# Attention with a mixture of experts, one core: waits that are already satisfied left out of the queues, and one bias folded into another at the start

## The chip, the cores and the metric

One NeuronCore of a Trainium2 chip runs the whole program. The metric is the device time of one execution in microseconds (us); lower is better.

## The reference, cut to what matters

Eight batches of 512 rows by 128 columns. Each row is normalised, and the result `xn` goes through two branches that are added to `x`:

```
xn = layernorm(x)
out = x + attention(xn) + ffn(xn)

attention: q, k, v = xn @ W_qkv (16 heads of 64), rotary embedding on q and k, causal softmax, @ W_out
ffn:       q, k, v = xn @ Wq + bq, xn @ Wk + bk, xn @ Wv + bv      (16 heads of 8)
           ctx = softmax(q k' / sqrt(8)) v
           attn_out = ctx @ Wo + bo
           x2 = xn + layernorm(attn_out) * g1 + be1
           gate = softmax(x2 @ Wg + bg); the two best of 8 experts: sum of gate * (x2 @ We + bexp)
           ffn = x2 + layernorm(that) * g2 + be2
```

The softmax rows of the FFN's attention sum to one. So `bv`, which is added to each row of v, comes out of that attention unchanged, and `ctx @ Wo + bo` is the same with v lacking its bias and `bo` replaced by `bo + bv @ Wo`.

## The kernel before

The work of each batch is cut into steps, each with a short name: `proj` (projection of 128 columns of q or k), `raw`, `swap`, `rope`, `hi` and `lo` (its way through ScalarE, a DMA and GpSimd), `sc` (scores), `max`, `exp`, `tp` and `tq` (transposes of the weights), `tpe` and `tqe` (their copies), `pv`, `rT`, `div` and `ao` for the causal attention; `fqk`, `fsm`, `fmax`, `fmT`, `fst`, `fexp`, `fv`, `fpv`, `fT` for the FFN's; `wo`, `gate`, `moe` for the rest. A table of times (`START`, `PERIOD`, `SHIFT`, `FIRST`, `LAST`) is written out by hand, and sorting it gives each engine a fixed order: 1250 steps for TensorE, 1166 for ScalarE, 1074 for VectorE, 432 for GpSimd. The steps of neighbouring batches are interleaved. The order is the same in both kernels.

Engines meet through semaphores. Every kind of step has one (`done[kind]`), which a step raises by one when it ends. `after(kind, ...)` gives the semaphore and the value that it has when the named step is done:

```python
def after(kind, *key):
    if (kind,) + key not in COUNT:
        return begun, 1
    return done[kind], COUNT[(kind,) + key]
```

A step waits with `engine.wait_ge(*after(...))` for each of its inputs and for whoever last used the buffer that it overwrites. On TensorE there are also the waits for the PSUM banks: `BEFORE[x]` names the steps that free them (lines 1181 to 1187). An instruction of an engine takes one wait with it; the others stand in instructions of their own in the engine's queue, up to two waits in each. The trace calls these EVENT_SEMAPHORE, and their line is that of a wait.

Many of these waits name a value that the same engine has already waited for. The step `fmT` waits for eight `fmax` of one semaphore, one after the other; `inv` for six `exp`; `sc` for `hi` and `lo` of q and of k, though GpSimd makes each `lo` after its `hi`; and the second `fpv` of a group waits for `fexp` values that an earlier bank wait covered.

Products with more than half precision are made of three matmuls (`split3`: high by high, low by high, high by low, lines 1166 to 1168) and, where there is a bias, a fourth of 128 rows by 128 columns that adds one row of the tile `biases`, picked by a column of `pick` (line 1170). Four steps use it: `fv` (bias `bv`, 4 such matmuls per batch), `wo` (`bo`, 4) and `moe` (`bexp`, 8 of 512 columns).

The start: SyncE loads x, the constants, Wq and Wk, the biases of q and k (line 679) and, when GpSimd has cleared `raw_bias`, `bexp`, `bv` and `bo` twice each (line 686). TensorE then does `xT`, `tt`, `proj`, `tb` (a transpose of the q and k biases, line 1196), `fqk`, `fv`. VectorE does `ln`, `turn`, `str`, `xn`, `strl`, `wl`, `xl`, `wl`, `sml`, `qkb` (lines 972 and 976, from the result of `tb`), `bia` (lines 990 to 993, `pick` and `biases`), `wel` (line 997), `fqkl` (line 1013).

Of the kernel before, what the change touches and what calls it, by code (L numbers as in the profile page):

```python
# [14 lines left out]
P = 128  # L15
# [17 lines left out]
BIAS = {"bexp": 0, "bv": 2, "bo": 3}  # L33
# [502 lines left out]
def build(nc, x, w_qkv, w_out, wq, bq, wk, bk, wv, bv, wo, bo, g1, be1, g2, be2, wg, bg, we, bexp, table, rope, out):  # L536
    with ExitStack() as ctx:
# [32 lines left out]
        spare = sb("spare", [P, 1])  # L570
        warm = sb("warm", [P, 1])
# [62 lines left out]
        columns_loaded = sem("columns_loaded")  # L634
        causal_loaded = sem("causal_loaded")
# [35 lines left out]
        def _(sp):  # L671
# [20 lines left out]
            for x_ in ORDER["SP"]:  # L692
                kind, b = x_[:2]
                if kind == "swap":
# [3 lines left out]
                    sp.wait_ge(*after("raw", b, c, k))  # L698
                    sp.wait_ge(*after("rope", old, older // 2, older % 2))
                    for r in range(2):  # L700
                        sp.dma_start(swapped[r:P:2, n % 2], raw[1 - r:P:2, n % 3]).then_inc(swap_done[n % 2], 16)
                elif kind == "store":
                    sp.wait_ge(*after("out", b))
# [8 lines left out]
        def _(pool):  # L712
# [16 lines left out]
            for x_ in ORDER["POOL"]:  # L729
                kind, b = x_[:2]  # L730
                if kind in ("rs0", "rs1", "rs2"):
                    n = int(kind[2])
                    pool.wait_ge(*after(("ln", "ln1", "ln2")[n], b))
                    nc.gpsimd.tensor_tensor(rstd[:, n], spread[:, n], power[:], ALU.pow).then_inc(done[kind], 1)
                elif kind == "rope":
                    c, k = x_[2:]
                    n = (b * NC + c) * 2 + k
                    pool.wait_ge(*after("raw", b, c, k))
                    if n == 0:
                        pool.wait_ge(*after("tab", 0))  # L740
# [6 lines left out]
                elif kind == "hi":  # L747
                    c, k = x_[2:]
                    n = (b * NC + c) * 2 + k
                    pool.wait_ge(*after("rope", b, c, k))  # L750
                    pool.wait_ge(*after("sc", *ring(2, b, c, NC), 2))
                    nc.gpsimd.tensor_copy(qk_h[:, c % 2, k], raw[:, n % 3]).then_inc(done["hi"], 1)  # L752
                elif kind == "lo":
                    c, k = x_[2:]
                    n = (b * NC + c) * 2 + k
                    pool.wait_ge(*after("hi", b, c, k))
                    nc.gpsimd.tensor_tensor(qk_l[:, c % 2, k], raw[:, n % 3], qk_h[:, c % 2, k].bitcast(F32),  # L757
                                            ALU.subtract).then_inc(done["lo"], 1)
                elif kind in ("x2", "out"):
                    n = 0 if kind == "x2" else 2  # L760
                    pool.wait_ge(*after("nm1" if kind == "x2" else "nm2", b))
# [11 lines left out]
                    else:  # L773
                        pool.wait_ge(*after("res", b))
                        nc.gpsimd.tensor_tensor(x_in[:, b % XB], branch[:], x_in[:, b % XB], ALU.add).then_inc(done["out"], 1)
                elif kind == "res":
                    pool.wait_ge(*after("x2", b))
                    pool.wait_ge(*after("yadd", b, 1))
                    nc.gpsimd.tensor_tensor(x_in[:, b % XB], xn[:, b % 2], x_in[:, b % XB], ALU.add).then_inc(done["res"], 1)

        @block.scalar
        def _(act):
# [12 lines left out]
            for x_ in ORDER["ACT"]:  # L795
                kind, b = x_[:2]
                if kind == "tab":
                    act.wait_ge(*after("tt", 0))
# [13 lines left out]
                elif kind == "xh":  # L812
                    act.wait_ge(*after("xT", b))
                    act.wait_ge(*after("proj", b - 2, NC - 1, 1))
                    act.wait_ge(*after("fqk", b - 2, G - 1))
                    act.wait_ge(*after("v", b - 2, T - 1))
                    nc.scalar.copy(xt_h[:, b % 2], bank_of(("xT", b))).then_inc(done["xh"], 1)
                elif kind == "fvc":
                    act.wait_ge(*after("fv", b))
                    act.wait_ge(*after("fpv", b - 1, G - 1, T - 1))  # L820
                    nc.scalar.copy(fv[:, :, :, 0:FD], bank_of(("fv", b)).rearrange("p (t h d) -> p t h d", t=T, d=FD))\
                        .then_inc(done["fvc"], 1)
                elif kind == "fqkh":
                    g = x_[2]
                    act.wait_ge(*after("fqk", b, g))
                    act.wait_ge(*after("fst", *ring(2, b, g, G), T - 1))
                    if b == 0:
                        act.wait_ge(*after("qkb", 0))
# [4 lines left out]
                elif kind == "fexp":  # L833
                    g, i, r = x_[2:]
                    act.wait_ge(*after("fst", b, g, i))
                    if b == 0:
                        for n in range(3):
                            act.wait_ge(*after("wl", 0, n))
                    old, older = ring(FP, b, g * T + i, G * T)
                    act.wait_ge(*after("fpv", old, older // T, older % T))  # L840
                    nc.scalar.activation(fpt[:, ((b * G + g) * T + i) % FP, 2 * r:2 * r + 2].rearrange("p h n -> p (h n)"), bank_of(("fst", b, g, i), 2 * r, 2),  # L841
                                         ACT.Exp, scale=1.0 / math.sqrt(FD)).then_inc(done["fexp"], 1)
                elif kind == "fo":
                    g = x_[2]
                    act.wait_ge(*after("fpv", b, g, T - 1))
                    act.wait_ge(*after("fT", *ring(1, b, g, G)))
                    nc.scalar.copy(fo[:], bank_of(("fpv", b, g, 0))).then_inc(done["fo"], 1)
                elif kind == "ch":
                    act.wait_ge(*after("cT", b))
                    act.wait_ge(*after("moe", b - 1, T - 1))  # L850
                    nc.scalar.copy(ct_h[:], bank_of(("cT", b))).then_inc(done["ch"], 1)
                elif kind == "x2h":
                    act.wait_ge(*after("x2T", b))
                    act.wait_ge(*after("wo", b))
                    nc.scalar.copy(ct_h[:], bank_of(("x2T", b))).then_inc(done["x2h"], 1)
                elif kind == "gexp":
                    act.wait_ge(*after("gsub", b))
                    act.wait_ge(*after("moew", b - 1, T - 1))
# [566 lines left out]
```

## Time and profile before

| | |
|---|---|
| median of 3 runs | 1279.72 us (1278.18 to 1283.24) |
| the profiled execution | 1279.87 us |
| its span, first to last instruction | 1277.9 us |
| busy: TensorE, VectorE, ScalarE, GpSimd | 1156.8, 928.2, 892.0, 818.0 us |
| mean granted TensorE clock | 0.981 |

The profiled execution is 1.97 us longer than its span, and 0.15 us longer than the median. In the profile PE is TensorE's matmul row, PEld its row of weight loads (which overlap matmuls), DVE is VectorE, ACT ScalarE, POOL GpSimd, SP SyncE; a name with a q behind it (PEldq, ACTq) is that engine's queue of instructions. Matmuls are pipelined, so the busy time of PE is larger than the time in which it could do no more. A number like L1267 is a line of the kernel.

### The profile page before, as it was taken

What the parts mean: (1) busy time and instruction counts of PE and PEld (TensorE: products, weight loads), DVE (VectorE), ACT (ScalarE), POOL (GpSimd) and SP (SyncE); (2) the same over time, 40 slices, a digit from 0 to 9 for tenths busy, and PEclk for the clock granted to TensorE, in tenths of its full rate; (3) what the DMA queues carried; (4) which work ended last, traced back from release to release, by engine and by line L of the source; (5) the groups of instructions that cost most, each with busy time, mean ns of one, the idle gap of its engine ahead of it and who ended that gap; (6) DMA issues with size and microseconds to landing.
All of it is one profiled execution on the core that took longest, in us unless ns stands there. A gap on an engine that the chain in (4) does not pass through costs nothing.

```text
span 1277.9 us, 28127 instructions
## 1 busy us (share of the span) xinstructions
PE 1156.8 (91%) x9417; PEld 739.4 (58%) x9417; DVE 928.2 (73%) x2328; ACT 892.0 (70%) x1841; POOL 818.0 (64%) x734
## 2 busy tenths in 40 slices
PE   4779999999899999999999999999999999899985
PEld 2354565656565565756656556655656556565553
DVE  8666477875878768885779848787678956778455
ACT  3577767587766868588775887668675786758760
POOL 3664774676855867468855678567675578536751
PEclk8799999999999999999999999999999999999988
DMA  5000100011000110001100111001100011000000
GB/s 143 34 34 18 43 34 18 26 51 35 26 26 18 51 43 26 17 35 51 42 9 34 34 37 40 18 26 51 43 26 17 26 47 38 18 30 22 35 17 9
DMA packets 33970, 43.05 MB, mean 34 GB/s; under 512 B 5536, under 2 KB 17060, under 8 KB 33832
## 3 DMA queue, kind: packets, MB, share of 16 engines
q1 hardware_dynamic: 30360, 38.31, 8.6%
q10 hardware_dynamic: 3472, 2.95, 0.8%
q8 instruction: 80, 1.31, 0.5%
q14 instruction: 58, 0.48, 0.1%
HBM read 5.60 MB, written 2.10 MB: 6 GB/s over the span
## 4 chain that ended last, share of the span: by engine, by line
PE 62%; ACT 13%; DVE 12%; issue 11%; POOL 1%; DMA 1%; DVEq 0%; ACTq 0%; POOLq 0%
PE work L1252 8%; PE work L1166 7%; PE work L1267 7%; PE work L1333 6%; PE work L1280 6%; PE work L1168 6%; PE work L1167 6%; DVE fnmax L1022 5%; ACT pn L883 5%; PE work L1296 4%; ACT fpt L841 4%; PE work L1305 4%; PE work L1322 3%; ACT pt L895 2%; ACT fqk L830 2%
## 5 line engine op out<-in xcount | busy, mean ns | idle before, releaser
L883 ACT ACTIVATE pn<-work,nmax 128x512 f32<-128x512 f32 (+3 forms) x512 | 265.3, 534 | 126.0 <-DVE nmax L1124 125.8
L742 POOL TENSOR_TENSOR raw<-raw,cos_t 128x512 f32<-128x512 f32 x128 | 164.2, 1282 | 293.6 <-DMA swapped<-raw 279.5
L1022 DVE TENSOR_REDUCE fnmax<-work 128x2 f32<-128x1024 f32 x256 | 301.6, 1218 | 48.3 <-PE work L1305 47.1
L1124 DVE CUSTOM_DVE_ANT_0 work<-work,causal 128x512 f32<-128x512 f32 (+3 forms) x512 | 236.2, 520 | 99.1 <-PE work L1252 98.8
L841 ACT ACTIVATE fpt<-work 128x1024 f32<-128x1024 f32 x256 | 252.3, 1028 | 55.2 <-PE work L1322 54.1
L1267 PE MATMUL work<-consts,pn 128*128 128x128 f32 x1280 | 172.1, 277 | 5.9 <-DVE fnmax L1022 3.7
L746 POOL TENSOR_TENSOR raw<-raw,swapped 128x512 f32<-128x512 f32 x128 | 163.9, 1280 | 10.0
L757 POOL TENSOR_TENSOR qk_l<-raw,qk_h 128x512 fp32r<-128x512 f32 x128 | 163.7, 1285 | 2.8
L1267 PEld LDWEIGHTS work<-consts,pn 128*128 128x128 f32 x1280 | 141.3, 141 | 40.6 <-DVE fnmax L1022 12.7
L743 POOL TENSOR_TENSOR swapped<-swapped,sin_t 128x512 f32<-128x512 f32 x128 | 164.0, 1282 | 0.0
L895 ACT COPY pt<-work 128x1024 f32<-128x1024 f32 x128 | 130.1, 1018 | 33.7 <-PE work L1267 33.1
L1280 PE MATMUL work<-pt,v 128*32 128x512 f32 (+3 forms) x2048 | 152.0, 438 | 0.0
L1333 PE MATMUL work<-fpt,fv 128*9 128x512 f32 x1024 | 132.4, 601 | 0.3 <-ACT fpt L841 0.3
L1280 PEld LDWEIGHTS work<-pt,v 128*32 128x32 f32 x2048 | 61.7, 110 | 94.3 <-issue 76.9
L1252 PE MATMUL work<-qk_h 64*128 64x512 f32 (+3 forms) x512 | 98.3, 375 | 13.5 <-ACT pt L895 6.4
L752 POOL CAST qk_h<-raw 128x512 fp32r<-128x512 f32 x128 | 78.0, 613 | 47.2 <-PE work L1252 44.4
L883 ACT ACTIVATION_READ_ACCUMULATOR pn<-work,nmax 128x1 f32 x512 | 107.2, 209 | 0.0
L866 ACT COPY raw<-work 128x512 f32<-128x512 f32 x128 | 75.4, 595 | 38.9 <-PE work L1168 34.7
L1305 PE MATMUL work<-fqk 32*128 32x512 f32 x512 | 66.0, 502 | 30.6 <-DVE branch L1107 7.4
L1322 PE MATMUL work<-fqk 32*128 32x512 f32 x512 | 65.3, 495 | 28.9 <-ACT pt L895 11.4
L1252 PEld LDWEIGHTS work<-qk_h 64*128 64x128 f32 x512 | 50.3, 187 | 63.6 <-issue 24.9
L1252 PE MATMUL work<-qk_l,qk_h 64*128 64x512 f32 (+3 forms) x512 | 85.4, 323 | 0.0
(154 smaller groups left out, 2142.7 us busy)
## 6 DMA issues: line engine op xcount, KB each, us to landing
swapped<-raw SPq DMA_DIRECT2D x256, 128.0 KB, 2.1
x_in<-in_L_attn_x_dram SPq DMA_DIRECT2D x8, 256.0 KB, 3.7
out_dram<-x_in SPq DMA_DIRECT2D x8, 256.0 KB, 2.3
fpt<-in_L_attn_W_qkv_dram ACTq DMA_DIRECT2D x3, 512.0 KB, 5.9
pt<-in_L_ffn_We_dram ACTq DMA_DIRECT2D x1, 512.0 KB, 7.3
wout<-in_L_attn_W_out_dram ACTq DMA_DIRECT2D x1, 512.0 KB, 8.8
pt<-in_rope_dram ACTq DMA_DIRECT2D x1, 192.0 KB, 6.7
affine<-in_L_ffn_g_dram SPq DMA_DIRECT2D x2, 64.0 KB, 4.6
```

The lines of the kernel that those rows point to most:

```text
L742: nc.gpsimd.tensor_tensor(raw[:, n % 3], raw[:, n % 3], cos_t[:], ALU.mult)
L743: nc.gpsimd.tensor_tensor(swapped[:, n % 2], swapped[:, n % 2], sin_t[:], ALU.mult).then_inc(pool_link, 1)
L746: nc.gpsimd.tensor_tensor(raw[:, n % 3], raw[:, n % 3], swapped[:, n % 2], ALU.add).then_inc(done["rope"], 1)
L757: nc.gpsimd.tensor_tensor(qk_l[:, c % 2, k], raw[:, n % 3], qk_h[:, c % 2, k].bitcast(F32), ALU.subtract).then_inc(done["lo"], 1)
L841: nc.scalar.activation(fpt[:, ((b * G + g) * T + i) % FP, 2 * r:2 * r + 2].rearrange("p h n -> p (h n)"), bank_of(("fst", b, g, i), 2 * r, 2),
L883: ins = nc.scalar.activation(pn[:, h, PN_AT[j]:PN_AT[j] + n], bank_of(("sc", b, c, unit), h)[:, at:at + n], ACT.Exp, scale=-1.0, bias=nmax ...
L1022: nc.vector.tensor_reduce(fnmax[:, j, 2 * r:2 * r + 2, 0:1], bank_of(("fsm", b, g, j), 2 * r, 2).rearrange("p (f n) -> p f n", f=2), AX.X, ...
L1124: ins = nc.vector.tensor_tensor_reduce(out=scores, in0=scores, in1=causal[:, S - n:S], scale=-1.0 / math.sqrt(DH), scalar=3.0e38, op0=ALU.add,
L1252: ins = nc.tensor.matmul(bank_of(x_, h)[:, at:at + (j + 1) * P], left[rows, c % 2, 0, tile(j)], right[rows, c % 2, 1, 0:(j + 1) * P], star ...
L1267: ins = nc.tensor.transpose(dst[:, at + (j - i) * P:at + (j - i + 1) * P], pn[:, h, from_:from_ + P], ident)
L1280: ins = nc.tensor.matmul(psum[a:a + STRIP, i * P:S], v[:, i, 2 * c + h, a % DH:a % DH + STRIP], pt[:, c % 2, h, PT_AT[i]:PT_AT[i] + S - i ...
L1333: ins = nc.tensor.matmul(psum[f * STRIP:f * STRIP + FVW], fv[:, i, g * GH + f], fpt[:, ((b * G + g) * T + i) % FP, f], start=i == 0, stop= ...
```

## The change

Each engine's waits go through a function that remembers, per engine and semaphore, the highest value already waited for. It leaves out a wait for no more than that, and of several waits given in one call for one semaphore it keeps the highest. `begun` falls under the same rule. Waits on DMAs and the links inside a step stay as they are. `sc` waits for the two `lo` alone.

```diff
+        passed = {}
+        def wait(engine, *steps):
+            most = {}
+            for semaphore, value in steps:
+                most[semaphore.name] = max((value, semaphore), most.get(semaphore.name, (0, semaphore)), key=lambda v: v[0])
+            for name, (value, semaphore) in most.items():
+                if passed.get((engine, name), 0) < value:
+                    passed[engine, name] = value
+                    engine.wait_ge(semaphore, value)
...
                     freed = [after(*y) for y in BEFORE[x_]]
-                    for n, (bank_free, value) in enumerate(freed):
-                        if (bank_free, value) not in freed[:n]:
-                            pe.wait_ge(bank_free, value)
+                    wait(pe, *freed)
...
                 elif kind == "fmT":
-                    for j in range(T):
-                        for r in range(2):
-                            pe.wait_ge(*after("fmax", b, g, j, r))
+                    wait(pe, *(after("fmax", b, g, j, r) for j in range(T) for r in range(2)))
...
-                        for k in range(2):
-                            pe.wait_ge(*after("hi", b, c, k))
-                            pe.wait_ge(*after("lo", b, c, k))
+                        wait(pe, after("lo", b, c, 0), after("lo", b, c, 1))
```

The second part takes `bv` out of `fv`. It is loaded as one column (`value_bias`, 128 packets of 4 bytes), `tb` multiplies it by Wo, spread over 128 identical rows, and `qkb` adds the row to `bo` in `raw_bias`. For this `tb` waits for two more loads, and `pick` is made in `qkb` instead of `bia`. The two loads of `bv` into `raw_bias` go.

```diff
-BIAS = {"bexp": 0, "bv": 2, "bo": 3}
+BIAS = {"bexp": 0, "bo": 2}
...
             sp.dma_start(causal[:, S - P:S], table[:, C_MS:C_MS + P]).then_inc(causal_loaded, 16)
+            sp.dma_start(value_bias[:], bv.rearrange("(d a) -> d a", a=1)).then_inc(value_bias_loaded, 16)
             sp.wait_ge(cleared_bias, 1)
-            for name, a in (("bexp", bexp.rearrange("e d -> (e d)")), ("bv", bv), ("bo", bo)):
+            for name, a in (("bexp", bexp.rearrange("e d -> (e d)")), ("bo", bo)):
...
                 elif kind == "qkb":
-                    dve.wait_ge(*after("tb", 0))
+                    dve.wait_ge(table_loaded, 16)
+                    nc.vector.tensor_tensor(pick[:], ident[:, 0:len(BIAS) + 1], ident[:, DH:DH + len(BIAS) + 1], ALU.add)\
+                        .then_inc(dve_link, 1)
+                    dve.wait_ge(dve_link, link())
+                    wait(dve, after("tb", 0))
+                    dve.wait_ge(bias_loaded, 16 * 5)
+                    nc.vector.scalar_tensor_tensor(out=raw_bias[:, 0:D], in0=bank_of(("tb", 0))[:, P:P + D],
+                                                   scalar=pick[:, BIAS["bo"]:BIAS["bo"] + 1].bitcast(F32), in1=raw_bias[:, 0:D],
+                                                   op0=ALU.mult, op1=ALU.add)
...
                 elif kind == "tb":
...
+                    pe.wait_ge(value_bias_loaded, 16)
+                    pe.wait_ge(small_loaded, 16 * 3)
+                    nc.tensor.matmul(psum[:, P:P + D], value_bias[:].broadcast_to([P, P]), raw_small[:, D:2 * D], start=True, stop=True)\
+                        .then_inc(done["tb"], 1)
...
-                        ins = split3(psum[:, tile(t)], xt_h[:, b % 2, tile(t)], xt_l[:, b % 2, tile(t)], small_h[:, 0:D], small_l[:, 0:D],
-                                     bias_of("bv"))
+                        ins = split3(psum[:, tile(t)], xt_h[:, b % 2, tile(t)], xt_l[:, b % 2, tile(t)], small_h[:, 0:D], small_l[:, 0:D])
```

## Rows read from the trace of the kernel before

**Rows 1.** The page: busy us (share of the span) and instructions of each engine.

```profile
PE 1156.8 (91%) x9417; PEld 739.4 (58%) x9417; DVE 928.2 (73%) x2328; ACT 892.0 (70%) x1841; POOL 818.0 (64%) x734
```

**Rows 2.** The page: the chain that ended last, by engine.

```profile
PE 62%; ACT 13%; DVE 12%; issue 11%; POOL 1%; DMA 1%; DVEq 0%; ACTq 0%; POOLq 0%
```

**Rows 3.** PE's waits: us in total, times, longest; first and last of 37.

```profile
PE work L1201 <- DVE xn L939: 12.1, 1, 12.1
...
PE work L1267 <- ACT pn L883: 0.2, 1, 0.2
```

**Rows 4.** Queue instructions by line: ns min/median/max, first and last start.

```profile
L1261 PEldq EVENT_SEMAPHORE  x649: 51/51/1959, 60.3 to 1242.3; - x163
...
L1312 PEldq EVENT_SEMAPHORE  x128: 51/51/51, 35.2 to 1186.8; - x128
...
L840 ACTq EVENT_SEMAPHORE  x256: 17/17/38, 36.3 to 1211.5; - x128
```

**Rows 5.** The chain in order of time, 640 to 655 us: start, us, what.

```profile
644.03 0.14 issue
644.17 0.53 PE work L1322 x4
644.70 0.02 issue
644.72 0.02 ACT fpt L841
...
646.67 0.04 issue
646.71 0.33 PE work L1166
```

**Rows 6.** Groups by line: busy, mean ns, idle before.

```profile
L1280 PE MATMUL work<-pt,v 128*32 128x512 f32 (+3 forms) x2048 | 152.0, 438 | 0.0
```

**Rows 7.** PE in order of time: start, us; two transposing steps of eight matmuls.

```profile
641.88 1.09 PE L1267 MATMUL work<-consts,pn 128*128 128x128 f32 x8
...
670.32 1.04 PE L1267 MATMUL work<-consts,pn 128*128 128x128 f32 x8
```

**Rows 8.** PE in order of time, inside the first `fv`.

```profile
19.44 0.28 PE L1168 MATMUL work<-small_l,xt_h 128*128 128x128 f32 x1
...
19.55 0.27 PE L1170 MATMUL work<-biases,pick 128*128 128x128 f32 x1
```

**Rows 9.** VectorE's waits for `exp` before `inv`, and one of them in order of time.

```profile
DVE l_inv L1143 <- ACT pn L883: 15.5, 16, 1.6
...
857.72 0.23 ACT L883 ACTIVATION_READ_ACCUMULATOR pn<-work,nmax 128x1 f32 x1
...
858.17 0.20 DVE L1143 RECIPROCAL l_inv<-l_sum 128x8 f32<-128x8 f32 x1 [1.58 <-ACT pn L883]
```

**Rows 10.** The start, in order of time: loads, `tb`, `qkb`, `wel`, `fqkl`.

```profile
8.43 0.55 SPq L686 DMA_DIRECT2D pt<-in_L_ffn_bv_dram  x2
...
9.28 0.41 ACT L808 CAST small_h<-pt 128x264 fp32r<-128x264 f32 x1 [0.76 <-DMA pt<-in_L_ffn_Wg_dram]
...
16.53 0.28 PE L1196 MATMUL work<-consts,pt 64*128 64x64 f32 x1
...
16.85 0.17 DVE L972 COPY qk_bias<-work 128x8 f32<-128x8 f32 x1 [0.45 <-PE work L1196]
...
17.32 0.15 DVE L990 TENSOR_TENSOR pick<-consts 128x4 fp32r<-128x4 f32 x1
...
18.52 1.22 DVE L997 TENSOR_TENSOR we_l<-pt,we_h 128x1024 fp32r<-128x1024 f32 x1
...
19.92 1.41 DVE L1013 SCALAR_TENSOR_TENSOR fqk<-work,qk_bias,fqk 128x512 fp32r<-128x512 f32 x2 [0.19 <-ACT fqk L830]
```

**Rows 11.** Stages: us, busy of PE, PEld, DVE, ACT, POOL, granted clock, DMA share, GB/s.

```profile
23.20:33.50 10.30, 5.89 (x21) 3.69 (x21) 8.54 (x8) 0.71 (x2) 4.88 (x5) 0.50 0.06 23
...
60.80:1235.00 1174.20, 1097.03 (x9073) 701.45 (x9065) 860.80 (x2157) 861.56 (x1793) 776.30 (x687) 1.00 0.09 32
```

More of the change, by code:

```diff
@@ L702, in _ @@
                 elif kind == "store":
-                    sp.wait_ge(*after("out", b))
+                    wait(sp, after("out", b))
                     sp.dma_start(out_tiles[b], x_in[:, b % XB]).then_inc(out_sent[b % XB], 16)
@@ L1026, in _ @@
                     g = x_[2]
-                    dve.wait_ge(*after("fmT", b, g))
+                    wait(dve, after("fmT", b, g))
                     nc.vector.tensor_tensor(fqk[:, g % 2, 0], bank_of(("fmT", b, g)), fqk[:, g % 2, 0].bitcast(F32),
@@ L1138, in _ @@
                     c = x_[2]
-                    for unit in range(3):
-                        for h in range(2):
-                            dve.wait_ge(*after("exp", b, c, unit, h))
-                    dve.wait_ge(*after("fan", *ring(1, b, c, NC)))
+                    wait(dve, *(after("exp", b, c, unit, h) for unit in range(3) for h in range(2)))
+                    wait(dve, after("fan", *ring(1, b, c, NC)))
                     nc.vector.reciprocal(l_inv[:], l_sum[:, c % 2]).then_inc(done["inv"], 1)
@@ L1259, in _ @@
                         if j >= min(i for i, _ in ST_UNITS[unit]):
-                            for h in range(2):
-                                pe.wait_ge(*after("exp", b, c, [n for n in range(3) if j in [a for a, _ in SM_UNITS[n]]][0], h))
+                            unit_of = [n for n in range(3) if j in [a for a, _ in SM_UNITS[n]]][0]
+                            wait(pe, after("exp", b, c, unit_of, 0), after("exp", b, c, unit_of, 1))
                             for i, at in ST_UNITS[unit]:
@@ L1285, in _ @@
                     c = x_[2]
-                    pe.wait_ge(*after("fan", b, c))
+                    wait(pe, after("fan", b, c))
                     for t in range(T):
@@ L1292, in _ @@
                     pe.wait_ge(wout_loaded, 16)
-                    pe.wait_ge(*after("div", b, half * (NC // 2) + NC // 2 - 1))
+                    wait(pe, after("div", b, half * (NC // 2) + NC // 2 - 1))
                     for t in range(T):
@@ L1301, in _ @@
                     if j == 0:
-                        pe.wait_ge(*after("fqkl", b, g))
+                        wait(pe, after("fqkl", b, g))
                     for f in range(GH):
@@ L1337, in _ @@
                     g = x_[2]
-                    pe.wait_ge(*after("fo", b, g))
+                    wait(pe, after("fo", b, g))
                     for t in range(T):
@@ L1347, in _ @@
                 elif kind == "wo":
-                    pe.wait_ge(*after("cl", b))
+                    wait(pe, after("cl", b))
                     for t in range(T):
```

222 lines of the change are left out of this document (110 added, 112 removed).

## The prediction

> **What bounds the kernel now.** I read the page first, for the busy shares and the chain, then the waits of PE, the queue instructions by line, and last the chain and the timeline piece by piece around a few steps, to see what a queue instruction costs where it stands. TensorE shows the highest busy time [rows 1], and more than half of the chain that ended last is PE's [rows 2]. The reader should see in both that no engine is full: PE's busy time leaves 121.1 us of the 1277.9 us span idle, and VectorE, ScalarE and GpSimd are at 64% to 73%. The chain passes between engines all the time; 11% of it is "issue", time in which nothing that the profile shows was waited for. PE waited for another engine 175 times (the sum over the 37 groups whose first and last are in [rows 3]), 99.8 us in all, 12.1 of them before the first transpose. So the kernel is bound by a fixed order in which PE mostly works and now and then meets a late ScalarE or VectorE. From 61 to 1235 us the granted clock is 1.00, the level of 2.4 GHz, and the busy rows of the stages look alike [rows 11]; what a batch gains, eight batches gain.
>
> **How many queue instructions go.** This is a count in the code, no time. Going through TensorE's order with the old rule gives 4235 waits; one goes with each instruction, two fit in each queue instruction, which makes some 1812 of these. The trace's own counts at the lines of waits bear the rule out, 649 at L1261 and 128 at L1312 [rows 4], four for each of the 32 `fmT`. With the new rule there are some 1470 waits and 360 queue instructions. VectorE goes from about 825 to 200, ScalarE from 1020 to 415, GpSimd from 275 to 210, SyncE stays.
>
> **What a queue instruction costs.** There are three cases.
>
> Where the engine is behind its queue, nothing. The step `pv` has four or five waits before its first matmul, and PE's L1280 shows 0.0 us idle before it over 2048 matmuls [rows 6]. The Trainium skill, page "TensorE: Matmul & The Clock Gate", section "Step-by-step: what each phase is for", says that the sequencer does not wait for a matmul to drain and takes up the next instruction at once. By that rule alone the waits that are left out give nothing; L1280 agrees with it.
>
> Where PE stands and waits, the end of the wait must pass through the queue. In one piece of the chain ScalarE ends at 646.67 and PE starts 0.04 us later; in another it ends at 644.03 and PE starts 0.14 us later [rows 5]. I read the difference, 0.10 us, as one or two queue instructions of 51 ns [rows 4] that come behind the release. For 175 stalls that bounds the gain at 17.5 us; the lower bound is nothing. Not all of it goes: the waits that are kept are those that name something new, so they are the late ones, and a stalled step often keeps two different semaphores and so a queue instruction. By the count in the code about half of the waiting steps keep as many as they have, and the others lose one. I take a quarter of the bound: 175 x 0.10 x 0.25 = 4.4 us.
>
> Inside a transposing step (L1267) waits stand between the matmuls. One step of eight took 1.09 us and another 1.04 [rows 7]. There are 128 such steps of eight; 128 x 0.05 = 6.4 us is the upper bound, nothing the lower. Most steps look nearer to the long one, but PE is on the chain for 62% [rows 2]; I take half, 3.2 us.
>
> On VectorE, `inv` waits for six `exp` and one `fan`. ScalarE's last read ends at 857.95 and `inv` starts at 858.17, 0.22 us later [rows 9]; 0.02 us is what ScalarE needs after PE's L1322 [rows 5]. So 0.20 us each, 16 times [rows 9]: 3.2 us at most. `inv` leads to `rT` and `div`, which have room in most batches, and it keeps one queue instruction; I take a third, 1.0 us. Nothing at all if `rT` is covered.
>
> The other waits of ScalarE, VectorE and GpSimd I cost at nothing. ScalarE's L840 takes 17 ns, 256 times, 4.4 us if all of it were bare [rows 4], yet ScalarE's L841 starts 0.02 us after PE ends, with such an instruction ahead of it [rows 5]: the queue instruction is done while the engine runs the operation before, or waits. That work of about 0.6 to 1 us is the cover; without it the 4.4 us is the bound, for ScalarE.
>
> **The bias.** In `fv` a fourth matmul is left out 4 times per batch, 32 in all. Inside `fv` one matmul starts 0.11 us after the last [rows 8], so 32 x 0.11 = 3.5 us less work of PE. It is gained where PE is on the chain, 62% of the time [rows 2]: 2.2 us, with 0 and 3.5 as bounds.
>
> **The start.** What is added lies in the first 20 us. SyncE issues one load of 128 small packets and two fewer; an issue takes about 0.3 us [rows 10], so the queue behind it (the biases, x of batches 1 and 2, the affine rows) moves by 0.3 us or less and earlier after that. `tb` waits for the value bias and for Wv, Wo and Wg. The last of these have landed when ScalarE casts them at 9.28 us, and `tb` runs at 16.53 [rows 10], so their wait is free by 7 us. The value bias is issued near 7.8 us; it would have to take nearly 9 us to be late. On PE `tb` gets one more matmul; a step of 128 columns starts the next after 0.11 us [rows 8] and I allow 0.2 us with its two waits, ahead of `fqk`, which ScalarE and then `fqkl` wait for. On VectorE `qkb` gets `pick` (0.15 us, moved from `bia`, and now before the wait for `tb`, so in the idle 0.45 us) and one multiply-add of 128 columns out of PSUM. No row before shows it; its bounds are 0.15 us, `pick` with 4 columns, and 0.71 us, half of the two 512-column operations of L1013 [rows 10]; between them 0.3, being the nearer in size to the small one. Queued behind it are `bia`, `wel` and `fqkl`. `wel` ended at 19.74 and `fqkl` started at 19.92 [rows 10], so 0.18 us of room; `bia` also waits for `qkb` of its own engine. Both chains come out at 0.2 to 0.6 us late. I take 0.5 us, bounds 0.1 and 1.5.
>
> **The sum.** 4.4 + 3.2 + 1.0 + 2.2 - 0.5 = 10.3 us less. The profiled execution took 1279.87 us for a span of 1277.9; so 1269.6 us, and 0.15 us less against the median of 1279.72: 1269.4, given as 1269.5. With all upper bounds (17.5 + 6.4 + 3.2 + 4.4 + 3.5 - 0.1 = 34.9) it is 1245; with all lower and the start at 1.5, 1281.
>
> **The rivals.** *The queue is hidden everywhere but for the bias.* Then 2.2 - 0.5 = 1.7 us is left: 1278. For it speaks L1280 [rows 6] and ScalarE's 0.02 us [rows 5]; against it the 0.14 us of [rows 5] and the 0.22 of [rows 9]. Chance 0.27, with every case in which the stalls that shrink are not those of the chain.
>
> *The queue is a bound of its own.* If PE's sequencer cannot keep ahead in the runs of short steps, the 1450 instructions of 51 ns each that go are 74 us of its time [rows 4]; at PE's share of the chain, 62% [rows 2], that is 46 us: 1234. Halfway between this and my sum, 1252, only short steps gain. Against it: 0.0 us idle at L1280. Chance 0.12 for anything under 1255.
>
> *The bias is covered.* The change's second half does nothing if `fv` lies where PE waits for `fexp` or `exp` anyway; then 1271.7. It is inside the likeliest case.
>
> *Slower by the clock.* PE does less and the same work is waited for. In the stage from 23.2 to 33.5 us PE was busy for 5.89 of 10.3 us and the granted clock was 0.50, the level of 1.2 GHz; in the long stage it is 1.00 [rows 11]. If a dip of 3.4 us to 1.2 GHz came back in every batch it would cost up to 1.7 us of matmuls each, 13.6 us for eight, and cancel the gain. Two dips per batch cost 27 us: 1269.5 + 27.2 = 1297. It decides from ten dips on, which is 17 us, more than 6.4 above the median. Against it: PE's share changes by under 1%. The Trainium skill, page "Perfetto Trace Analysis", section "Matmul Optimizations", says that the matmul engine scales its power with its use, so matmuls should run back to back; that is the rule that speaks against less work on PE. Chance 0.04. In a fixed order a removed delay makes no other step later, so apart from the clock only the start can lose time, and there 1.5 us is the bound; 0.02 for something unseen there, such as a late value bias.
>
> **How the numbers follow.** A difference of 0.5%, 6.4 us, is about what a measurement of this kernel can tell from none. The likeliest case, 1259 to 1273, has 0.55; hidden, 1273 to 1280, has 0.27; the queue as a bound, under 1255 or near it, 0.12; slower 0.06. Faster by over 0.5% means under 1273.3: 0.55 + 0.12 = 0.67, less 0.02 for the edge: 0.65. The same 0.29, slower 0.06. The range takes in both neighbours and leaves out the far ends, 0.1 below 1252 and 0.1 above 1278.
>
> **What would show it.** PE's queue instructions fall to about 360, those at L1312's successor to nearly none. PE's waits fall by about 5 us in total at the same count, and the chain's 0.14 us pieces before L1322 become 0.04. Transposing steps of eight take 1.04 us. The matmuls on `biases` are 96 instead of 128, and each `fv` ends 0.44 us earlier after its start. `inv` starts within 0.1 us of `exp`. In the start `fqkl` begins at 20.1 to 20.5 instead of 19.92. I am wrong if the busy sum of PE shrinks but its idle time grows by as much, which is the hidden case; if L1280, L1252 or L1305 become shorter step by step, the queue was a bound; if the mean granted clock of the long stage falls to 0.99 or less, the clock took it back.

## The result, and the profile after

| | before | changed |
|---|---|---|
| median, run by turns on one chip (8 runs each) | 1283.31 us (1278.18 to 1285.48) | 1275.38 us (1273.78 to 1282.10) |
| the profiled execution, and its span | 1279.87, 1277.9 us | 1276.25, 1274.5 us |
| mean granted clock of the profiled execution | 0.981 | 0.977 |
| queue instructions of TensorE, VectorE, ScalarE, GpSimd, SyncE | 1814, 827, 1023, 278, 131 | 361, 204, 418, 213, 130 |

The ratio is 0.9946 [0.9931, 0.9962]: 0.54% faster, about 6.9 us (5 to 9), where 10.3 us had been forecast. The absolute forecast of 1269.5 us started from a median of three runs, 1279.72; with more runs the kernel before stands 3.6 us higher, so the ratio is the fairer measure of the sum, and by it the forecast gain was half as large again as the measured one. 1275.38 is inside 1252 to 1278. Taken as it stands it lies in the stretch of the hidden case (1273 to 1280), and 0.54% is just over the 0.5% that the prediction took as its line.

Lines moved with the edit: L1252 is now L1271, L1267 L1286, L1280 L1298, L1305 L1323, L1322 L1338, L1333 L1348, L1166 to L1170 L1185 to L1189, L841 L856, L883 L898, L895 L910, L1143 L1162. All merged waits stand at L669.

The page of the changed kernel, busy times and the chain by engine:

```profile
PE 1156.8 (91%) x9387; PEld 737.4 (58%) x9387; DVE 926.7 (73%) x2329; ACT 891.6 (70%) x1841; POOL 817.6 (64%) x734
...
PE 56%; DVE 15%; ACT 14%; POOL 6%; issue 6%; DMA 2%; SPq 0%; POOLq 0%; ACTq 0%; DVEq 0%
```

Against [rows 2] "issue", time in which the chain waits for nothing that the profile shows, fell from 11% to 6%. PE's busy sum is that of [rows 1] to the tenth although matmuls are gone: what that hides comes below. The queue instructions at the line of merged waits (ns min/median/max, first and last start):

```profile
L669 ACTq EVENT_SEMAPHORE  x415: 17/17/2982, 9.1 to 1244.0; - x139
L669 PEldq EVENT_SEMAPHORE  x350: 51/51/1457, 11.8 to 1252.1; - x175
L669 DVEq EVENT_SEMAPHORE  x175: 21/21/50, 9.4 to 1253.3; - x175
L669 SPq EVENT_SEMAPHORE  x127: 17/17/17, 13.4 to 1202.5; - x127
L669 POOLq EVENT_SEMAPHORE  x80: 17/17/17, 7.3 to 1269.1; - x80
```

They last what they lasted in [rows 4], 51 ns on PE and 17 on ScalarE; there are fewer of them. Groups by line, with the idle time before them; the second is the bias matmul:

```profile
L1298 PE MATMUL work<-pt,v 128*32 128x512 f32 (+3 forms) x2048 | 152.2, 438 | 0.0
...
L1189 PE MATMUL work<-biases,pick 128*128 128x512 f32 (+1 forms) x96 | 35.7, 372 | 0.0
```

L1298, the counterpart of [rows 6], did not change and still has 0.0 us idle before it: nothing shows that the waits ahead of `pv` had cost anything. The bias matmuls are 96 instead of 128. The chain of the changed kernel at the place of [rows 5] (start, us, what):

```profile
640.56 1.02 ACT pt L910
641.58 0.14 issue
641.72 0.53 PE work L1338 x4
642.27 1.95 ACT fpt L856 x2
```

This is the piece that was to shrink to 0.04 us. It is still 0.14. The start in order of time, beside [rows 10]:

```profile
17.20 0.35 DVE L992 SCALAR_TENSOR_TENSOR pt<-work,pick,pt 128x128 f32<-128x128 f32 x1 [0.92 <-DVE pick L987]
...
20.32 1.41 DVE L1034 SCALAR_TENSOR_TENSOR fqk<-work,qk_bias,fqk 128x512 fp32r<-128x512 f32 x2
```

The added multiply-add took 0.35 us, and `fqkl` starts at 20.32 instead of 19.92. TensorE and its clock in stretches of the changed kernel (us, busy of PE, PEld, DVE, ACT, POOL, granted clock, DMA share, GB/s):

```profile
60.80:1235.00 1174.20, 1100.45 (x9061) 702.68 (x9054) 860.96 (x2168) 861.30 (x1793) 776.31 (x688) 0.99 0.09 31
...
228.10:231.50 3.40, 1.92 (x13) 1.09 (x13) 2.75 (x3) 2.43 (x3) 0.00 (x0) 1.00 0.21 80
231.50:234.90 3.40, 3.40 (x12) 2.71 (x11) 2.75 (x3) 0.00 (x0) 3.20 (x3) 0.50 0.00 0
979.00:982.40 3.40, 3.40 (x10) 2.55 (x10) 2.26 (x2) 0.47 (x1) 0.27 (x1) 0.51 0.16 55
1132.60:1136.00 3.40, 3.40 (x10) 2.56 (x10) 2.30 (x3) 0.00 (x0) 2.69 (x3) 0.51 0.02 6
```

And the same kind of rows around the first of these places before the change:

```profile
229.50:232.90 3.40, 1.93 (x13) 1.18 (x14) 2.76 (x3) 2.37 (x3) 0.14 (x1) 1.00 0.21 77
232.90:236.30 3.40, 3.40 (x19) 2.77 (x18) 3.37 (x4) 0.00 (x0) 3.32 (x3) 1.00 0.00 0
```

The long stage is at 0.99 where it was at 1.00 [rows 11], and its PE busy sum is 3.4 us larger with fewer matmuls. Three stretches of 3.4 us at 0.50, the level of 1.2 GHz, are most of why; the rest is the fall at the end of the work, which starts at 1231.6 us, inside the long stage, and at 1235.0, behind it, before the change. In both kernels a pause goes before the place near 230 us (PE busy for 1.92 and 1.93 of 3.4 us); before the change the clock stayed at 1.00 behind it, after it fell. Each of the two profiles has two more such falls, near 95 and 170 us.

The fall near 230 us doesn't come of the change. The kernel before with a single step of VectorE altered (inv_one_wait, below) has it too, behind the same pause:

```profile
230.10:233.50 3.40, 1.91 (x13) 1.05 (x12) 2.75 (x3) 2.43 (x3) 0.00 (x0) 1.00 0.21 77
233.50:236.90 3.40, 3.40 (x11) 2.73 (x10) 2.68 (x3) 0.00 (x0) 3.10 (x3) 0.50 0.00 0
```

The profile before is of an execution with few falls: it took 1279.87 us at 0.981, and of the 73 runs of the same kernel beside the experiments only two were as short, with a mean clock of 0.979. So the pair of profiles shows a larger difference of the clock (0.981 and 0.977) than the runs do.

The end of the last `pv` of one batch to that of the next, read from the traces, in us:

```
         first pv group ends   seven batch lengths                             end
before   209.6                 150.6 150.4 150.4 150.6 150.2 152.9 134.8       1277.9
changed  208.7                 150.9 149.2 149.9 149.2 149.0 153.8 135.7       1274.5
```

A batch without a fall went from about 150.4 to 149.2 or 149.3, 1.1 to 1.2 us less. One with a fall lasted 150.9. The last two, each with one fall more than before, came out 0.9 us longer.

### The profile page after: what moved, and what is told of

Its sections match the earlier page's. It is cut to its first block, busy times and chain, and to the rows that moved or that the text cites. A ratio compares the mean times of both kernels' runs of the same rounds, so it can differ in the third digit from the quotient of the medians.

```text
span 1274.5 us, 25320 instructions
## 1 busy us (share of the span) xinstructions
PE 1156.8 (91%) x9387; PEld 737.4 (58%) x9387; DVE 926.7 (73%) x2329; ACT 891.6 (70%) x1841; POOL 817.6 (64%) x734
## 4 chain that ended last, share of the span: by engine, by line
PE 56%; DVE 15%; ACT 14%; POOL 6%; issue 6%; DMA 2%; SPq 0%; POOLq 0%; ACTq 0%; DVEq 0%
PE work L1271 7%; PE work L1185 7%; PE work L1286 6%; PE work L1298 5%; PE work L1187 5%; PE work L1186 5%; PE work L1348 5%; ACT fpt L856 5%; DVE fnmax L1043 4%; PE work L1314 4%; ACT pn L898 4%; DVE work L1145 3%; PE work L1323 3%; PE work L1338 3%; ACT pt L910 2%
## 5 line engine op out<-in xcount | busy, mean ns | idle before, releaser
L898 ACT ACTIVATE pn<-work,nmax 128x512 f32<-128x512 f32 (+3 forms) x512 | 265.3, 534 | 123.2 <-DVE nmax L1145 123.0
L856 ACT ACTIVATE fpt<-work 128x1024 f32<-128x1024 f32 x256 | 252.4, 1029 | 52.7 <-PE work L1338 51.3
L1286 PE MATMUL work<-consts,pn 128*128 128x128 f32 x1280 | 173.0, 277 | 6.2 <-DVE fnmax L1043 4.0
L761 POOL TENSOR_TENSOR raw<-raw,swapped 128x512 f32<-128x512 f32 x128 | 163.9, 1280 | 10.0
L1286 PEld LDWEIGHTS work<-consts,pn 128*128 128x128 f32 x1280 | 141.2, 141 | 41.7 <-DVE fnmax L1043 13.1
L910 ACT COPY pt<-work 128x1024 f32<-128x1024 f32 x128 | 130.2, 1019 | 32.6 <-PE work L1286 32.1
L1298 PE MATMUL work<-pt,v 128*32 128x512 f32 (+3 forms) x2048 | 152.2, 438 | 0.0
L1348 PE MATMUL work<-fpt,fv 128*9 128x512 f32 x1024 | 132.6, 602 | 0.3 <-ACT fpt L856 0.3
L1298 PEld LDWEIGHTS work<-pt,v 128*32 128x32 f32 x2048 | 61.7, 110 | 94.6 <-issue 77.0
L1271 PE MATMUL work<-qk_h 64*128 64x512 f32 (+3 forms) x512 | 97.9, 375 | 13.2 <-ACT pt L910 6.6
L898 ACT ACTIVATION_READ_ACCUMULATOR pn<-work,nmax 128x1 f32 x512 | 107.2, 209 | 0.0
L1338 PE MATMUL work<-fqk 32*128 32x512 f32 x512 | 65.1, 496 | 28.7 <-ACT pt L910 12.9
L1323 PE MATMUL work<-fqk 32*128 32x512 f32 x512 | 66.0, 502 | 27.0 <-DVE branch L1128 7.5
L1271 PEld LDWEIGHTS work<-qk_h 64*128 64x128 f32 x512 | 49.9, 187 | 63.6 <-issue 22.2
L1271 PE MATMUL work<-qk_l,qk_h 64*128 64x512 f32 (+3 forms) x512 | 84.8, 323 | 0.0
```

Of the source, the lines that this page charges most:

```text
L761: nc.gpsimd.tensor_tensor(raw[:, n % 3], raw[:, n % 3], swapped[:, n % 2], ALU.add).then_inc(done["rope"], 1)
L898: ins = nc.scalar.activation(pn[:, h, PN_AT[j]:PN_AT[j] + n], bank_of(("sc", b, c, unit), h)[:, at:at + n], ACT.Exp, scale=-1.0, bias=nmax ...
L1271: ins = nc.tensor.matmul(bank_of(x_, h)[:, at:at + (j + 1) * P], left[rows, c % 2, 0, tile(j)], right[rows, c % 2, 1, 0:(j + 1) * P], star ...
L1286: ins = nc.tensor.transpose(dst[:, at + (j - i) * P:at + (j - i + 1) * P], pn[:, h, from_:from_ + P], ident)
L1298: ins = nc.tensor.matmul(psum[a:a + STRIP, i * P:S], v[:, i, 2 * c + h, a % DH:a % DH + STRIP], pt[:, c % 2, h, PT_AT[i]:PT_AT[i] + S - i ...
L1348: ins = nc.tensor.matmul(psum[f * STRIP:f * STRIP + FVW], fv[:, i, g * GH + f], fpt[:, ((b * G + g) * T + i) % FP, f], start=i == 0, stop= ...
```

## The experiments

Every ratio is to the kernel before, run by turns with it on the same chip, with its 95% interval. The kernel before had a median of 1282.76, 1282.99 and 1282.78 us in the three sets, so it moved by less than 0.3 us between chips.

### Set 1: the two parts, and the waits engine by engine

**waits_only**: the change with the old bias kept.

```diff
-BIAS = {"bexp": 0, "bo": 2}
+BIAS = {"bexp": 0, "bv": 2, "bo": 3}
...
-                        ins = split3(..., small_h[:, 0:D], small_l[:, 0:D])
+                        ins = split3(..., small_h[:, 0:D], small_l[:, 0:D], bias_of("bv"))
```

> The merged waits alone; the bias of the values stays in fv as in the kernel before. Theory A (queue instructions behind a release cost PE 51 to 100 ns, and this is most of the gain): 4 to 7 us faster than before, ratio 0.995 to 0.997, nearly as fast as the changed kernel. Rival B (queue instructions are hidden, the gain came from the 32 matmuls): within 1 us of before, ratio 1.000.

Measured: 0.9969 [0.9957, 0.9981], median 1279.05 us, 3.7 to 4.0 us less.

**bias_only**: the change with every `wait(engine, ...)` turned back into one wait per step named.

```diff
+        def wait_all(engine, *steps):
+            seen = []
+            for semaphore, value in steps:
+                if (semaphore.name, value) not in seen:
+                    seen.append((semaphore.name, value))
+                    engine.wait_ge(semaphore, value)
```

> The folded bias alone; every wait is issued as in the kernel before. Theory A: PE has 3.5 us less work, of which some 2 us are on the chain, and the start costs up to 0.5 us: 1 to 2.5 us faster, ratio 0.998 to 0.999. Rival B: all of the changed kernel's gain is here, about 7 us, ratio 0.9945. Rival C (the start costs more than the matmuls bring): 1.000 or above.

Measured: 0.9989 [0.9980, 0.9997], 1281.87 us, 1.4 us less (0.4 to 2.6).

**waits_pe_only** and **waits_others_only**: the merged waits on TensorE alone, and on every other engine alone; the old bias in both.

```diff
-wait(dve, ...)    # and act, pool, sp; in the other kernel: pe
+wait_all(dve, ...)
```

> Waits merged on PE's queue alone, old bias, all other queues as before. Theory A: PE is the only engine whose stalled steps start later for a queue instruction (135 ns against 43 ns after the release), so this has nearly all of what the merged waits give: 3.5 to 7 us faster, ratio 0.995 to 0.997. Rival D (VectorE's inv with its six waits, and the other queues, carry it): under 1 us faster.

> Waits merged on the queues of VectorE, ScalarE, GpSimd and SyncE, PE's as before, old bias. Theory A: 0 to 1.5 us faster, the part of inv (16 stalls of at most 0.20 us). Rival D: 3 us faster or more.

Measured: 0.9981 [0.9969, 0.9993], 1281.57 us, and 0.9982 [0.9973, 0.9991], 1280.83 us. By the ratios that is 2.4 and 2.3 us.

What follows from the four: the parts add up within their intervals. 2.4 and 2.3 us of waits make 4.7 against 4.0 measured together, and 0.9969 x 0.9989 is 0.9958 against 0.9946 for the whole. By the ratios waits are about three quarters of the gain and the bias a quarter; the batches without a fall, read behind set 3, give the bias more. 1454 queue instructions fewer on TensorE gave 2.4 us, 1.7 ns each, where each lasts 51 ns: most were hidden.

### Set 2: is it their number or their place?

From the semaphore updates in the traces I worked out, for each step of TensorE between 60 and 1200 us that had to wait, the time from the release to the first matmul. It takes few values. When the late wait is the first that the step names, it is 43 or 44 ns. When another wait is named first, the late one stands in a queue instruction, and it is 90 or 135 ns, up to 246 with several behind. Time over 43 ns, summed: 15.4 us before, 8.9 us changed, nearly all in 94 steps that still name two or three semaphores with the late one not in front. Of these sums 7.0 and 4.0 us lie in steps before which PE's row shows idle time, and 4.6 us in waits_pe_only; in the others the row still shows the matmul before. Merging drops waits that are satisfied, but not this order.

**late_first_pe**: the changed kernel, where the wait that ended last in its trace is issued ahead of a step's other waits; none is added or taken away. A table written out per step of TensorE (145 entries) says which. **late_first_all**: the same for VectorE (76), ScalarE (27) and GpSimd (29), and `rope` waits for `raw` behind its DMA.

```diff
+LATE = {"PE": {0: ("xn", 1), 5: ("bia", 1), 6: ("fqkl", 1), 7: ("fmax", 1),
...
+            for at, x_ in enumerate(ORDER["PE"]):
+                if at in LATE["PE"]:
+                    last, value = LATE["PE"][at]
+                    wait(pe, (done[last], value))
```

> The changed kernel, and on PE the wait that ended last in its own trace is now issued first, so that it goes with the step's first instruction and not in a queue instruction ahead of it; 145 of 1250 steps get another order of waits, no wait is added or dropped otherwise. Theory A (the place of the late wait decides): steps that started 135 ns after their release now start 43 ns after it; 94 such stalls of the changed kernel hold 8.3 us, of which the chain should pass on half or more, so 3 to 7 us faster than the changed kernel, ratio to before 0.989 to 0.992. Rival (only the number of queue instructions counts): as the changed kernel, 0.9945.

> The same on PE, VectorE, ScalarE and GpSimd, and rope waits for the swapped rows' DMA before it waits for raw. VectorE's late waits in a queue instruction cost 92 ns against 23, 29 times, GpSimd's about 55 to 70 more, some 70 times with the swap. Theory A: 1 to 3 us faster than the one for PE alone. Rival: those stalls are covered, the same as for PE alone.

Measured: 0.9937 [0.9921, 0.9954], 1275.61 us, and 0.9935 [0.9912, 0.9958], 1273.26 us. The queue instructions are 361 on PE as in the changed kernel, and the time over 43 ns falls from 8.9 to 1.2 us (with idle time before the step, from 4.0 to 0.4). Against 0.9946 for the changed kernel in another set the intervals overlap, so this alone decided nothing; set 3 runs them side by side.

**more_waits**: the kernel before with two more waits, long satisfied, behind the bank waits of each TensorE step that has any.

```diff
+                    if freed:
+                        pe.wait_ge(begun, 1)
+                        pe.wait_ge(begun, 1)
```

> The kernel before with two more waits, for a semaphore that was satisfied long ago, at each PE step that takes a PSUM bank from another step: some 1100 more queue instructions on PE, nothing else changed. Theory A (queue instructions cost only behind a late release): 2 to 6 us slower than before, ratio 1.002 to 1.005. Rival 'hidden': 1.000. Rival 'the queue is a bound of its own': 1100 times 51 ns is 56 us, at PE's share of the chain 35 us, ratio 1.027.

Measured: 1.0022 [1.0008, 1.0036], 1285.68 us. TensorE has 2963 queue instructions instead of 1814. 1149 more of 51 ns are 59 us of its queue and cost 2.7 us, 2.3 ns each, near the 1.7 ns that the opposite gave. With the queue a bound of its own this would have been 62% of 59 us, 36 us. That rival is excluded.

**no_value_bias**: the kernel before with the fourth matmul of `fv` left out and nothing added, so its output lacks `bv`.

```diff
-                                     bias_of("bv"))
+                                     )
```

> The kernel before without the 32 matmuls that add the values' bias, and without anything in their place: it leaves the bias of the values out of the result. All waits as before. Against the folded bias alone (ratio 0.9989) it shows what the added work at the start costs. Theory: 0.5 us, so 0.998 to 0.999. Rival (the start costs 2 us or more and hides the gain): 0.997 or below.

Measured: 1.0007 [0.9995, 1.0019], 1284.81 us. 32 matmuls fewer, no gain of the whole. Its profiled execution shows falls of the clock at two places where the profile of the kernel before has none:

```profile
830.80:834.20 3.40, 3.40 (x11) 2.42 (x8) 2.36 (x2) 0.93 (x2) 1.59 (x2) 0.50 0.21 77
1086.80:1090.20 3.40, 3.40 (x22) 2.93 (x22) 1.59 (x9) 2.38 (x8) 3.32 (x4) 0.50 0.21 77
```

### Set 3: side by side

**changed_again** is the changed kernel unaltered, **late_first_all_again** is late_first_all unaltered.

> The changed kernel unaltered, on the same chip as the next. It should repeat its 0.9946 within 0.993 to 0.996. Its granted clock should again be 0.001 to 0.002 below that of the kernel before, if the clock takes part of the gain back; at the same clock it would be 8 to 9 us faster.

> The changed kernel with the late wait issued first on PE, VectorE, ScalarE and GpSimd, again. Theory A (a late wait in a queue instruction costs 92 ns on PE and the chain passes it on): 2 to 4 us faster than the changed kernel beside it, ratio to before 0.991 to 0.993. Rival (the clock, or the last two batches, take it back): the same as the changed kernel within 1 us.

Measured: 0.9947 [0.9930, 0.9964], 1275.99 us, and 0.9906 [0.9887, 0.9924], 1270.58 us. The same 361 queue instructions, in another order, are 5.4 us apart, and the two intervals do not meet. It is the fastest version: 12.2 us under the kernel before. In set 2 the same kernel gave 0.9935, at a mean granted clock of 0.9747 against 0.9768 here, only 0.1% under the changed kernel. The pair side by side, 0.4%, is the fairer comparison, but it rests on five runs of one and nine of the other; the size is not settled, the sign is shown by this pair and by the batches below. The chain of late_first_all_again at the place shown above:

```profile
637.82 1.11 PE work L1367 x8
638.95 1.02 ACT pt L985
640.01 0.54 PE work L1419 x3
640.57 1.95 ACT fpt L931 x2
```

638.95 + 1.02 = 639.97, and PE's L1419 (L1338 of the changed kernel) starts at 640.01: 0.04 us in place of 0.14. The step has the same three waits as there, in another order.

**more_matmuls**: the kernel before with two more bias matmuls, of a row of zeros, in each group of `fv`: 64 more.

```diff
+                    for zero in more:
+                        nc.tensor.matmul(dst, zero[0], zero[1], start=False, stop=False)
```

> The kernel before with two more matmuls of a row of zeros for each of the 32 on the values' bias: 64 more, 7.0 us more work of PE at 0.11 us each. Theory P (PE's work is passed on by its share of the chain, 62%): 4.4 us slower, ratio 1.0034. Rival Q (fv lies where PE would wait anyway, so matmuls there are free both ways): 1.000 to 1.001. Rival R (all of it is passed on): 1.0055.

Measured: 1.0074 [1.0052, 1.0096], 1291.98 us, 9.2 us more, where 64 x 0.11 = 7.0 us is their own time. The stretch from 60 us to the end of the first `pv` group, before and in this kernel:

```profile
60.00:210.00 150.00, 134.56 (x1110) 82.58 (x1110) 100.56 (x241) 111.16 (x233) 94.50 (x85) 0.98 0.08 30
```

```profile
60.00:217.00 157.00, 141.65 (x1140) 87.51 (x1138) 102.68 (x247) 113.98 (x238) 96.01 (x87) 0.95 0.08 28
```

That group ends 7.5 us later (217.1 against 209.6) at a clock of 0.95 instead of 0.98, with two batches' `fv`, 16 matmuls or 1.8 us, behind it. Of the seven later batches the first five grow by 2.4, 1.7, 0.8, 0.9 and 1.1 us, the next by 1.1, the last not at all, where 8 x 0.11 = 0.9 us was added to each but the last. So even this is not a clean price of a matmul: the clock in the first 200 us took part of the profiled execution's time. Over the runs the mean clock was nearly the same (0.9783 against 0.9789), so the clock doesn't explain why the whole cost more than 7.0 us; that stays open.

**inv_one_wait**: the kernel before, with `inv` waiting for the last of its six `exp` only.

```diff
-                    for unit in range(3):
-                        for h in range(2):
-                            dve.wait_ge(*after("exp", b, c, unit, h))
+                    dve.wait_ge(*max((after("exp", b, c, unit, h) for unit in range(3) for h in range(2)), key=lambda w: w[1]))
```

> The kernel before with inv on VectorE waiting for the last of its six exp alone; nothing else merged. Theory A: inv starts within 0.1 us of its release instead of 0.22, 16 times, and a third of that reaches the end: 0.5 to 1 us, ratio 0.9993 or so, not to be told from none. Rival D (inv carries what the merged waits outside PE gave, 0.9982): 2 us faster or more.

Measured: 0.9996 [0.9985, 1.0008], 1282.15 us. VectorE has 699 queue instructions instead of 827. In order of time:

```profile
859.95 0.23 ACT L883 ACTIVATION_READ_ACCUMULATOR pn<-work,nmax 128x1 f32 x1
860.21 0.20 DVE L1141 RECIPROCAL l_inv<-l_sum 128x8 f32<-128x8 f32 x1 [1.38 <-ACT pn L883]
```

ScalarE ends at 860.18, `inv` starts 0.03 us later; in [rows 9] it was 0.22. The edit did what it should at `inv`, and the end of the kernel did not move clear of the noise.

**Batches without a fall.** The batch lengths, read as in the section on the result, make the comparison without the clock. Of the five batches from the end of the first `pv` group on, these are the ones in which the granted clock stayed at 1.00, one profiled execution of each kernel:

```
                        lengths, us                      mean
before                  150.6 150.4 150.4 150.6 150.2    150.4
inv_one_wait            150.4 150.3 150.5 150.1          150.3
waits_others_only       150.2 150.3 150.2 150.1          150.2
no_value_bias           150.4 149.9 149.9 150.1          150.1
bias_only               149.8 149.8 149.9                149.8
waits_pe_only           149.7 150.1 149.7                149.8
waits_only              149.8 149.9 149.6 149.6          149.7
changed                 149.2 149.9 149.2 149.0          149.3
changed_again           149.2 149.2                      149.2
late_first_all_again    149.4 148.4 148.8                148.9
more_waits              150.4 150.6 150.9                150.6
more_matmuls            152.1 151.2 151.5 151.3          151.5
```

The bias matmuls, 4 x 0.11 = 0.44 us of a batch, gave 0.4 and 0.6 us when they went, and twice as many more cost 1.1. PE's waits gave 0.6 us a batch, those of the other engines 0.2, the order of the waits 0.3 more. Two kernels that lack the same matmuls, no_value_bias and bias_only, differ by 0.3 here, so 0.2 is not told from nothing. So what no_value_bias gained in these batches its other batches lost again: the fifth, with a fall, is 1.2 us longer than before, the sixth 3.4, the seventh 1.1. One fall doesn't explain the 3.4; that stays open.

## Why the prediction was right, point by point

**Right in kind.** Faster, by a little over half a per cent; the number of queue instructions (360, 200, 415, 210 forecast; 361, 204, 418, 213 counted); L1280 unchanged; the start later by 0.40 us where 0.5 had been taken, with the multiply-add at 0.35 for 0.3. The load of `bv` landed in time. PE's waits were to fall by about 5 us in total and fell from 99.8 to 94.8, though the count went from 175 to 156. (The groups behind the 175 are 38, not 37.)

**Waits: 8.6 us forecast, 4.0 measured [2.4, 5.5].** Term by term:

- *Stalls of PE, 4.4 us.* The mechanism is shown: a late wait that sits in a queue instruction costs 90 to 246 ns, in front 43. The time so lost on PE fell by 15.4 - 8.9 = 6.5 us, more than my 4.4, since I had priced a quarter of the stalls at 0.10 us each, and the long ones of 196 to 246 ns are gone. But that also counts steps before which PE's row shows no idle time. My 175 were stalls with idle time, and there it fell by 7.0 - 4.0 = 3.0 us, in waits_pe_only by 2.4. PE's merged waits alone gave 2.4 us [0.9, 4.0], and that includes the next term. The step was therefore sized too high by about 2 us (0.4 to 3.5). My test for it failed outright: the 0.14 us before L1322 (now L1338) stayed, because that step keeps waits on three semaphores and names the late one behind.
- *Transposing steps, 3.2 us.* This term was nothing. Over all steps of eight transposes that the timeline shows as one piece between 60 and 1240 us, the mean was 1.065 us before (88 pieces, 40 of them 1.09) and 1.064 us changed (89 pieces, 41 of them 1.09). The waits between the matmuls went; the 1.09 stayed. What makes the difference between 1.03 and 1.09 is open. I had read the difference between two rows as the price of waits without asking whether the step of the shorter row was without them; by the code both have them.
- *`inv`, 1.0 us.* Measured by itself: 0.5 us [-1.0, 1.9], and not told from nothing, though its 0.19 us per step did go. I had named that case ("nothing at all if `rT` is covered"); the interval leaves both it and my 1.0 us standing.
- *The other waits, costed at nothing.* Merged waits on all engines but PE gave 2.3 us [1.2, 3.5]. The intervals of this and of `inv` overlap, so that something was there that I left out is likely and not shown. ScalarE started 22 to 24 ns after the release in 332 of 348 stalls before, which bears out the zero for ScalarE. VectorE's late waits took 79 or 122 ns in queue instructions against 23 in front, GpSimd's 120 to 138 against 54 to 70. But merging left the stalls with the late wait in a queue instruction as many as they were on ScalarE (8 and 8) and GpSimd (73 and 72), so at their stalls the 2.3 us is not to be found. Where it comes from was not separated; the batches without a fall are 0.2 us shorter, no more than they can tell.

**Bias: 2.2 - 0.5 = 1.7 us forecast, 1.4 measured [0.4, 2.6].** The number is right; its reason is not. Leaving the matmuls out with nothing added should have shown the 2.2 us and showed -0.9 [-2.4, 0.6]. Adding 64 cost 9.2 us, more than their own time. I had let the chain's share, 62%, pass on their time. In batches without a fall it is passed on in full: 0.4 to 0.6 us for 0.44, 1.1 for 0.88. By that, as an estimate from 32 x 0.11, the matmuls were worth about 3.5 us, my upper bound; the rest of the kernel, batches with falls among it, took back part of it. So the 1.4 against 1.7 is in part luck.

**The rivals.** *Hidden but for the bias* (0.27): that would be 0.9987; the measured 0.9946 excludes it, and waits_only shows why, yet it is half true: of 51 ns per instruction, 1.7 to 2.3 ns counted. *Queue a bound of its own*: excluded by more_waits. *The bias covered*: that part would be 1.0004 (0.5 us of the start), just outside the [0.9980, 0.9997] of bias_only, though the ratio of no_value_bias alone would bear it out; its batches without a fall speak against it. *Slower by the clock*: wrong in sign, right that the clock takes part. The long stage fell from 1.00 to 0.99, the bound that the prediction had named, by three falls in the profiled execution, not the ten that it would have taken. In set 3 the mean granted clock was 0.9767 for the changed kernel and 0.9789 before. A straight line of time against clock through the runs of each set, with one level per kernel, gives 0.5, 0.7 and 0.9 us for 0.001 of clock; 0.0022 is then 1.1 to 1.9 us. Without it the gain would have been 8 to 9 us. This is an adjustment by regression, not an experiment: no run held the clock and changed the waits. The Trainium skill, page "Perfetto Trace Analysis", section "Matmul Optimizations", has the matmul engine scale its power with its use; that a fall follows a stretch in which PE was busy for 1.92 of 3.4 us agrees with it, and that the same pause had no fall behind it in the profile of the kernel before, yet had one in that of inv_one_wait, shows that it does not decide alone.

So the 10.3 us forecast became 6.9: 3.2 us were a term that does not exist, about 2 us of the stalls were not there to be had, 1 to 2 us may have gone to the clock, and up to 2.3 us came from waits that I had put at nothing. The two parts measured apart make 5.4 us, 1.5 less than the whole, which their intervals allow. The forecast was right in direction and in its mechanism at a stall; that the sum came as near as it did is partly luck, since a term too many and a term too few stood against each other.

## What to carry to other kernels

Ask of a wait not only whether it is needed but where it stands: the wait that ends last should be the first that the step names, since the reordering, with the same count, gave 5.4 us in one set and 1.4 us in another, and dropping 1454 instructions on TensorE gave 2.4. Compare stretches in which the clock did not fall before a small difference of the whole is explained: 1.2 us a batch was plain there, where single runs of one kernel lie 5 us and more apart. Count instructions to find what changes, but price them only at stalls, from the time between release and start, and only where that stall is on the chain. Before a difference between two rows is called the price of something, see whether one of the rows is without it.

## What the runs showed of the hardware

- On TensorE, from the release of a wait to the first matmul: 43 or 44 ns if it is the first that is named, 90 or 135 ns if it stands in a queue instruction (most of the changed kernel's 94 at 135), 196 to 246 ns in steps with more of them. The steps of 45 to 61 ns are close to the 51 ns of one queue instruction.
- VectorE: 23 ns in front, 79 to 122 in a queue instruction, 218 for `inv` with seven waits. GpSimd: 54 to 70, and 120 to 138. ScalarE: 22 to 24 in nearly all, 77 to 83 in a queue instruction (seven times before).
- The granted clock falls to 1.2 GHz for 3.4 us at the same place of a batch in some batches and not in others, and two executions of one kernel differ in it. Between 200 and 1200 us the first profile of the changed kernel has falls at 231.5, 979.0 and 1132.6 us; the second, changed_again, at 229.9, 530.3, 680.5, 980.8 and 1134.4, one or two batches apart:

```profile
229.90:233.30 3.40, 3.40 (x11) 2.48 (x8) 2.36 (x2) 0.31 (x1) 2.20 (x2) 0.50 0.10 39
...
680.50:683.90 3.40, 3.40 (x11) 2.42 (x8) 2.36 (x2) 0.95 (x2) 1.59 (x2) 0.50 0.20 77
```

There a batch with a fall lasts about 150.7 us and one without 149.2 (read from its trace as above), so one fall costs some 1.5 us, a fifth of what the whole change gave.
